# Adaptive-norm attention and quantised feed-forward: the second token tile's value projection issued four key tiles sooner, and the next input's tangent cut into four pieces among the first head group's last exponentials

## What is computed

```python
x = x + attention(cond(x, fside, fside, w1, u1, cond_512), w_qkv, w_o)
x = x + ffn(cond(x, fside, fside, w2, u2, cond_512), w_gate, w_up, w_down)
# cond: two decaying scans over the tokens (forward, backward) of exp(min(k,30)) and of that times v,
#       out = sigmoid(r) * num / max(den, 1e-8) * gain
# attention: 16 heads of 32 channels, causal softmax(q k^T / sqrt(32)) v, then w_o
# ffn: silu(gate) * up, both products and w_down on block-quantised operands
```

## Time and profile before

| | us |
|---|---|
| median of 3 runs (lowest, highest) | 894.74 (894.42, 895.02) |
| the profiled execution's own time | 893.81 |
| its span, first to last instruction | 892.0 |
| TensorE busy | 752.1 |
| VectorE busy | 771.5 |
| ScalarE busy | 468.5 |
| GpSimd busy | 73.5 |
| mean granted TensorE clock | 0.946 of full |

### The profile page before, as it was taken

One profiled execution on the slowest core, in us unless ns is written; L12 is line 12 of the kernel. 1 busy time (PEld: TensorE's weight loads), 2 busy tenths in 40 slices (PEclk: granted clock), 3 DMA queues, 4 the chain that ended last, 5 costly groups with the idle time before them and its releaser, 6 DMA issues.

```text
span 892.0 us, 10809 instructions
## 1 busy us (share of the span) xinstructions
PE 752.1 (84%) x3948; PEld 388.6 (44%) x3985; DVE 771.5 (86%) x1122; ACT 468.5 (53%) x710; POOL 73.5 (8%) x149
## 2 busy tenths in 40 slices
PE   4667649698789999987899999887999998988695
PEld 1222224345444444554444444554444444653583
DVE  4999999998998879989988799799897998643787
ACT  4965644368574461585654614757636226552340
POOL 1000001102100002111000021110000211100000
PEclk9786778799999999999999999999999999999798
DMA  9623311455200004763010037540100284400001
GB/s 334 256 82 106 106 59 38 98 123 155 60 25 24 1 12 118 201 164 86 15 34 1 12 94 200 155 118 12 36 1 12 58 212 120 95 2 0 1 1 47
DMA packets 31252, 73.06 MB, mean 82 GB/s; under 512 B 5856, under 2 KB 6880, under 8 KB 29408
## 3 DMA queue, kind: packets, MB, share of 16 engines
q1 hardware_dynamic: 19584, 46.67, 17.6%
q0 software_dynamic: 6144, 16.79, 8.0%
q10 hardware_dynamic: 5472, 8.92, 3.2%
HBM read 34.61 MB, written 4.19 MB: 44 GB/s over the span
## 4 chain that ended last, share of the span: by engine, by line
PE 51%; DVE 28%; issue 8%; ACT 7%; DMA 4%; POOL 1%; SPq 1%; ACTq 0%; DVEq 0%
PE bank L1530 9%; PE bank L1337 7%; PE bank L1425 6%; PE bank L1542 5%; PE bank L1414 4%; PE bank L1329 4%; DVE negmax L1061 4%; PE bank L1396 3%; DMA stacks<-rows 3%; PE bank L1441 2%; ACT region L558 2%; PE bank L1363 2%; DVE num L963 2%; PE bank L1398 2%; DVE fn L949 1%
## 5 line engine op out<-in xcount | busy, mean ns | idle before, releaser
L324 POOL DMA_DIRECT2D stacks<-rows x128 | 69.5, 551 | 699.3 <-DVE region L840 343.0
L558 ACT ACTIVATE region<-bank 128x384 f32<-128x384 f32 (+1 forms) x192 | 96.1, 523 | 58.5 <-PE bank L1399 55.9
L1396 PE MATMUL bank<-stacks 128*128 128x512 f32 (+3 forms) x256 | 104.7, 416 | 21.5 <-ACT region L558 21.3
L1337 PE MATMUL bank<-h,wqkv 128*128 128x512 f32 x256 | 115.6, 603 | 4.2 <-DVE region L1290 4.2
L1061 DVE TENSOR_REDUCE negmax<-bank 128x4 f32<-128x512 f32 (+2 forms) x96 | 98.5, 1035 | 23.6 <-PE bank L1370 12.2
L1363 PE MATMUL bank<-stacks 128*128 128x128 f32 (+3 forms) x256 | 79.2, 403 | 13.1 <-DVE negmax L1061 6.2
L1337 PEld LDWEIGHTS bank<-h,wqkv 128*128 128x128 f32 x256 | 48.6, 194 | 61.7 <-issue 55.6
L1398 PE MATMUL bank<-maxrow,pick 128*128 128x384 bf16 (+3 forms) x236 | 72.5, 307 | 0.0
L1396 PEld LDWEIGHTS bank<-stacks 128*128 128x128 f32 x256 | 49.7, 194 | 51.2 <-ACT region L558 41.8
L1329 PE MATMUL bank<-wqkv,h 128*128 128x512 f32 x128 | 60.8, 619 | 4.7 <-DVE h L997 4.7
L1583 PE MATMUL bank<-region,ident 128*128 128x512 f32 x64 | 48.5, 916 | 12.0 <-DVE identb L894 12.0
(11 more groups left out here) (182 smaller groups left out, 1482.9 us busy)
## 6 DMA issues: line engine op xcount, KB each, us to landing
stacks<-rows SPq DMA_DIRECT2D x128, 128.0 KB, 4.0
stacks<-rows POOLq DMA_DIRECT2D x128, 128.0 KB, 4.7
kt<-in_fside ACTq DMA_DIRECT2D x30, 256.0 KB, 3.4
region<-in_w_gate SPq DMA_DIRECT2D x4, 1024.0 KB, 11.1
h<-in_x SPq DMA_DIRECT2D x4, 1024.0 KB, 5.7
xt<-in_x SPq DMA_DIRECT2D x4, 1024.0 KB, 8.0
region<-in_w_up SPq DMA_DIRECT2D x4, 1024.0 KB, 5.5
region<-in_w_down SPq DMA_DIRECT2D x4, 1024.0 KB, 4.7
```

The source lines that it names most:

```text
L324: eng.dma_start(stacks[HD * r:HD * r + HD, at:at + 2, i, :].bitcast(F32), rows[mine, q:k + 1:k - q, :]).then_inc(stacked[s][i], 16)
L558: nc.scalar.activation(probs[:, i, P_AT[tiles[0]]:P_AT[tiles[0]] + columns], bank[4 + n % 2][:, 0:columns], ACT.Exp, scale=SCALE).then_inc ...
L1337: mm = nc.tensor.matmul(qk_banks(g)[s][:, :], wqkv[:, j, C * s + P * g:C * s + P * g + P], h[:, j, :], start=(j == 0), stop=(j == CJ - 1))
L1396: nc.tensor.matmul(o, ks[s][:, i, P * t:P * t + P], qs[s][:, i, P * t:T], start=True, stop=False, skip_group_check=True)
```

## The change

Three edits in the turn, and one wait that follows from them:

- TensorE issues `project_values(b, 1)` behind n = 3 in place of n = 7.
- ScalarE loads the exponential-and-tangent table ahead of exponential 8, where it was loaded behind the two `weigh`. The number of table loads stays.
- The tangent is four instructions of 512 elements, one each behind exponentials 8 (and the copy of the values, which moves there as well), 9, 10 and 11. The last turn has no tangent and no load.
- VectorE's wait for the tangent counts four for each turn.

```diff
+            def next_tanh(b, j):
+
+                act.wait_ge(h_in, b * 16 + 32)
+                nc.scalar.activation(h[:, j, :], h[:, j, :], ACT.Tanh, scale=0.5).then_inc(tanh_ready, 1)
+
             def turn(b, more):
...
                 load_k(b, 2)
                 reciprocals(b, 2)
                 own_exp(b, 3)
-                exps(b, 0, 8, 12)
+                if more:
+                    table(0)
+                exps(b, 0, 8, 9)
                 copy_values(b, (1,))
+                for j in range(CJ):
+                    if j:
+                        exps(b, 0, 8 + j, 9 + j)
+                    if more:
+                        next_tanh(b, j)
                 weigh(b, 3, 0)
                 weigh(b, 3, 1)
-                if more:
-                    table(0)
-                    act.wait_ge(h_in, b * 16 + 32)
-                    nc.scalar.activation(h[:, :, :], h[:, :, :], ACT.Tanh, scale=0.5).then_inc(tanh_ready, 1)
                 copy_maxima(b, 1)
                 if more:
                     table(6)
...
-                    dve.wait_ge(tanh_ready, n + 1)
+                    dve.wait_ge(tanh_ready, CJ * n + 1)
...
-                        if g == 0 and n == 7:
+                        if g == 0 and n == 3:
                             project_values(b, 1)
```

## The result

The changed kernel takes 926.41 us (median of 4 runs, 923.57 to 928.21), the kernel before 894.58 in the same session: a ratio of 1.0357 with a 95% interval of 1.0332 to 1.0382. The profiled execution of the changed kernel took 923.57 us, with a span of 921.8 where it was 892.0. It is slower, as forecast, but by twice as much, and outside the range of 902 to 914.

The account below looks back on a forecast made before the run. Bound: the stretch to the third group's first maximum, with ScalarE a link beside VectorE (86% busy) and TensorE (84%). Turns lose 3.9 + 4.2 + 2.5 + 1.5 = 12.1 us, clock 3.2, together 15.3: 894.74 to 910.0 us, range 902 to 914.

Parts of the forecast that it names:

- the wait for h: ScalarE's first tangent waits for the load of h, 1.1 us in each of three turns, bounds 0 and 1.5.
- Rival 4: Load of h much later, taking 8 us beside kt and stacks: 2.6 us more in three turns, 918 us; chance 0.08.
- The projection's shift: On TensorE, slot 2 ends 3.4 us later; through VectorE, den and ScalarE's reciprocals come 2.7 us later.
- The projection's price: In the last turn, without load or tangent, the third group's first maximum comes about 1.5 us late.
- The table load: On ScalarE, 1.28 us right ahead of exponential 8, which TensorE's piece 10 waits for; no longer covered behind exponential 11.
- Tangents among the exponentials: On ScalarE, four tangents at 0.54 us each in a row, three ahead of exponential 11, which ends 5.7 us later.
- The clock: TensorE falls to the lower clock after standing: 1.1 us a turn, 3.2 us for three turns, bounds 0 and 5.7.
- the sum without wait and clock: Third group's first maximum late by 3.9, 4.2 and 2.5 us in three turns, less the 1.1 us wait in each.
- Nothing is won back later: TensorE, ScalarE and VectorE leave the stretch through the third group's first maximum; their lateness there is not recovered further on.
- Rival 2: Head 3's stacks land alone, clear of the load; three turns win 1.3, 1.0 and 2.7 us, 889.7 us; chance 0.04.

Follow-up runs that it names:

- e1: Kernel before with only the value projection moved behind n = 3, ScalarE's order as it was; 910.68 us against 891.66, ratio 1.021.
- e3: Changed kernel with tangents reading another tile and ScalarE waiting for h only behind the second copy of maxima; input's tangent left out; 908.38 us, ratio 1.0193.
- e10: Kernel before with head 1's four stacking DMAs held on SP until the projection is over, load of h right behind; 909.3 us against 893.04, ratio 1.0181.
- e4: Changed kernel with SP issuing the load of h ahead of head 1's four stacking DMAs; 908.58 us, ratio 1.019 to the kernel before.
- e6: Changed kernel with SP holding the load of h until own_exp of unit 3 has ended; 924.77 us in one execution, kernel before 892.71.
- e9: Kernel of e7 with the projection also moved behind n = 3; 894.05 us against 893.04 for the kernel before, ratio 1.001.
- e7: Kernel before with h loaded after the third group's slot 0, table loads and tangent moved to the third copy of maxima; 890.75 us against 892.71, ratio 0.997.
- e8: Kernel before with only the table load moved ahead of exponential 8, tangent and projection unmoved; 892.88 us against 892.71, ratio 1.0008.

## Why the prediction was wrong

**The step that failed** is "the wait for h", by its number: "It took 5.4 to 5.8 us; I take 5.4, as GpSimd's DMAs crowd it less". It took 10.4 to 10.9, and GpSimd's DMAs crowd its end (0.44 MB against SP's 0.16 from 205 to 209). The prediction had seen that SP's queue would issue the load right behind head 1's stacks, and had the moment right; it took the duration from a row in which the load is issued 2.8 us after the last of them, and took the traffic of the other queues for lighter, which it was not. Four kernels that issue it right behind take 8.5 to 12.2 us (changed, e1, e3, e10), one that issues it ahead 5.3, one on another queue 6.6, one 2.2 us behind 7.2, and those that issue it well clear of them 4.7 to 6.5. e4 and the changed kernel differ in nothing but this order (the load is then issued at 6.26 in place of 10.42), e6 and the changed kernel in nothing but the gap; e10 has it slow with the engines' lists of before, though among more of GpSimd's stacks. That a load issued there is slow, and that waiting for it made the loss, is shown. What makes it slow is not. The wait was 6.2 us a turn in place of 1.1, 15.3 more in three turns, of the 16.4 that lie between 910.0 and 926.4.

Rival 4 was this mechanism, with 8 us as its price and 0.08 as its chance. It had been judged by three landings that lie within 0.4 us of each other; these were three repetitions of one order of the queue, and said nothing of another.

**The steps that held**, in the first turn, from the first exponential:

- Reciprocal predicted at 9.8, measured 9.84; exponential 8 at 13.75, measured 13.82. The projection's shift and its way through VectorE to ScalarE were right.
- The projection's price with nothing else in its way was 1.5 us in the last turn, measured 1.27 there and 1.1 a turn by e9 against e7.
- The table load cost what was said: 1.28, hidden when alone (e8), paid when the projection has taken the idle (exponential 8 1.40 later than in e1). The Trainium skill, page "ScalarE: Activation LUTs", section "Terms", has about 2.7 us for it. The trace does not agree: the load at 201.05 takes 1.28, and exponential 8 starts at 202.34, right at its end.
- Tangents among the exponentials: exponentials 9 to 11 lie at the predicted distances once the first tangent starts (2.54 us from the start of exponential 9 to the end of 11, predicted 2.5).
- The clock fell to 0.50. e4, without the wait for h, is 3.75, 4.70 and 3.45 us later than the kernel before in the three turns where the sum without wait and clock gives 2.8, 3.1 and 1.4. The rest, 0.95, 1.6 and 2.05 us, is 1.5 a turn where 1.1 was taken, within its bounds of 0 and 1.9 at the mean and over them in the third turn. That these remainders are all the clock's was not shown apart.
- Nothing is won back later: 161.6, 161.6 and 162.6 us for the rest of the turn before and after.

Rival 2's price, 1.3, 1.0 and 2.7 us for a load that stays clear of head 3's stacks, was measured by e7 as 1.07, 0.75 and 2.46; its mechanism is real, and the change only moved the load to a worse place.

## What to carry to other kernels

The landing time of a DMA is not its own alone: the same 1 MB took 5.1 to 12.2 us here. Before moving one, look at what is issued in the microseconds around it, on the same queue first and on the others too, and take no duration from a row with other neighbours. Here a large load that is needed late did best behind the small ones that are needed soon: that, and putting the tangent where ScalarE waits anyway, gave 0.3% where the change lost 3.6%. And an engine at half load can still be a link: read the idle time between its instructions in that stretch before adding to it.

## What the runs showed that was not expected

- A 1 MB load issued on a hardware queue directly behind four 128 KB stacking DMAs lands in 8.5 to 12.2 us, clear of them in 4.7 to 6.5, and the issue itself takes 0.58 to 1.04 us on SP in place of 0.34. Why is open. The load's own queue, the order of issue over all queues, and sharing the 16 engines with GpSimd's stacks were not told apart; a kernel that holds GpSimd's stacks of head 2 back until the load has landed would test the last. The DMA records have no engine number, so that it could not be seen which of the 16 came late.
- The slow load is not slow alone. In e1 and e10 the third group was late because TensorE waited for GpSimd's stacks of head 3 (up to 9.0 and 9.6 us, 6.2 at most before), not because anything waited for `h`.
- One load and four stacks in two orders of one queue, all else alike, are worth 15 us of 926 (31.8 over the kernel before for the changed kernel, 16.9 for e4).
